# The first and second attention in one order of ticks, and the seams behind the second attention reordered

## Chip, core and metric

The kernel runs on one core of one Trainium2 chip. The metric is the device time of one execution in microseconds (us); the time before is the median of three runs. One more execution was profiled, and all rows of the trace come from that one.

## What is computed

A chain of four cross-attention blocks over x (8 sequences, 128 x 256) and a context of the same shape, all in fp32:

```python
x = L0(x, ctx)   # per (batch, head): softmax(q k) -> mean and deviation of v; out = instance_norm(x) * std + mean
x = L1(ctx, x)   # keys from [ctx, x]; 16 heads; then rmsnorm, gelu MLP, + residual
x = L2(x, ctx)   # layernorm, cross attention (16 heads of 128, one bias key), twice; then layernorm, MLP
x = L3(x, ctx)   # layernorm, cross attention, layernorm, gelu MLP
```

L0's deviation is `sqrt(relu(softmax @ (v*v) - mean*mean))`. L1 takes L0's output both as latents (queries, part of the keys) and as residual, so its projections need L0's rows of the batch at hand and no others.

## The kernel before

Every engine runs the same list of events, made by Python generators, and picks out its own part of each event; so the order of the list is the order of every engine's queue. TensorE (PE) multiplies, ScalarE (ACT) does exponentials and one half of the PSUM copies, VectorE (DVE) maxima, reciprocals and the other half, GpSimd (POOL) scales the probabilities, adds rows and clears buffers, SyncE (SP) issues the DMAs. A dense product in fp32 accuracy is three matmuls of rounded parts (helper `three`, lines 686 to 690), so L688, L689 and L690 are most of PE's work whatever the stage.

- **First attention (L0)**: `l0_order` puts events at ticks. Ticks 0 to 127 have one score unit S each; X (transposed scores, their exp is line 1292) follows nine ticks later, then PV (line 1026), N and OUT for the mean and second moment, and `vr` (lines 1796 to 1798) for the variance. Only when all is done come the `fin` events: per pair of rows a square root on ACT (line 1271), a product on POOL (line 1802), a sum and a mask on DVE (lines 1644 and 1645), and the transposes `nT lat` (line 711) that make L1's input.
- **Second attention (L1)**: `att_order("L1")`, a plain sequence behind L0: a head of dense products and stackings (dk, dq, dv, pq, pk), then 64 units S, T, PV (score line 800, exp 1155, scaling on POOL 1718, transpose 812, product 833), OUT and the output product WO after every 16 units, and the norm's steps nS (statistics, sqrt), nX (scaling), nT (transposes). `zero_keys` and `zero_values` (lines 1722, 1723, 1726) clear buffers of L1 on POOL behind `fin`. DVE runs it through `late`, which puts a few kinds of event behind the next score.
- **MLPs**: `mlp_order`: up and down products; a down's bank is one of the two general banks (`j_bank`, `j_full`, `j_take`), which all dense products share in turn and which are handed on only when the last user has emptied them.
- **Wide attention (L2)**: `wide_order`: 16 pairs of heads, eight units S (line 881), T (890), PV (903) each. The products q, k and v of pair p+1 and the output product WO of pair p-1 fill the ticks of pair p. Pairs 7 and 15 end a layer (`last`).
- **Third MLP and last attention (L3)**: `mlp_order("L2")`, `att_order("L3")`, `mlp_order("L3")`. `take` (lines 1081 and 1350) splits a loaded weight pack into its two rounded parts.
- Banks: L0's scores use PSUM banks 0, 1, 5, X 2 and 3, PV 4; L1 uses 0 and 1 for scores, 2 and 3 for transposes, 4 and 5 for outputs; 6 and 7 are the general banks.

## Time and profile before

| | before |
|---|---|
| median of 3 runs | 1208.99 us (1207.41 to 1210.04) |
| the profiled execution | 1209.98 us, its span 1208.2 us |
| mean granted TensorE clock | 0.964 of full speed |
| busy: PE, PEld, DVE, ACT, POOL | 1073.6, 947.2, 747.4, 731.9, 319.4 us |

PE is the matmul engine, PEld its weight loads, which overlap. The granted clock is 1.00 at 2.4 GHz and 0.50 at 1.2 GHz. "Idle" in a row's brackets is the engine's idle time just before that row, with what ended it.

### The profile page before, as it was taken

How to read it: one execution, taken by the hardware profiler on the slowest of the kernel's cores; microseconds unless marked ns; L12 is line 12 of the kernel's file. 1: busy time of each engine (PE TensorE's matmuls, PEld its weight loads, DVE VectorE, ACT ScalarE, POOL GpSimd, SP SyncE). 2: the span in 40 equal slices, each digit the busy share in tenths (PEclk: the TensorE clock that was granted, in tenths of full speed). 3: DMA queues.
4: the chain of work that ended last, by engine and by line, in shares of the span. 5: the costliest groups of instructions: out<-in, count | busy, mean ns of one | idle time of the engine just before them, and what ended most of it. 6: DMA issues, size and time to landing. Idle time of an engine off the chain costs nothing.

```text
span 1208.2 us, 23834 instructions
## 1 busy us (share of the span) xinstructions
PE 1073.6 (89%) x8224; PEld 947.2 (78%) x8224; DVE 747.4 (62%) x1777; ACT 731.9 (61%) x2114; POOL 319.4 (26%) x435
## 2 busy tenths in 40 slices
PE   3799995899978999999999889999999789688788
PEld 3577773777757989999999869999999679566688
DVE  4777775687886645555555745555555666566773
ACT  1577774678885446665666556666655442688842
POOL 5334335456441003211111112111111211243410
PEclk9899997999998999999999999999999889799899
DMA  6111110000001021100011111111001110100000
GB/s 202 26 28 45 45 28 36 1 1 2 19 19 44 19 88 45 42 29 26 37 45 66 45 44 45 44 45 44 32 28 40 36 36 1 36 2 19 19 10 27
DMA packets 20412, 43.65 MB, mean 36 GB/s; under 512 B 3395, under 2 KB 10821, under 8 KB 20294
## 3 DMA queue, kind: packets, MB, share of 16 engines
q1 hardware_dynamic: 20294, 42.12, 10.5%
q8 instruction: 68, 1.11, 0.4%
q14 instruction: 50, 0.41, 0.1%
HBM read 36.87 MB, written 1.05 MB: 31 GB/s over the span
## 4 chain that ended last, share of the span: by engine, by line
PE 69%; DVE 13%; ACT 9%; issue 6%; POOL 3%; DMA 0%; SPq 0%; DVEq 0%; ACTq 0%; POOLq 0%
PE ps L688 15%; PE ps L689 14%; PE ps L690 14%; PE ps L903 4%; PE ps L881 4%; PE ps L1026 2%; ACT pt L1155 2%; PE ps L890 2%; PE ps L812 2%; DVE nm L1667 2%; PE ps L1013 2%; PE ps L1004 1%; PE ps L833 1%; PE ps L769 1%; DVE nmax L1491 1%
## 5 line engine op out<-in xcount | busy, mean ns | idle before, releaser
L1718 POOL TENSOR_TENSOR pt<-pt,prec 128x256 f32<-128x256 f32 (+1 forms) x224 | 181.3, 810 | 650.4 <-DVE prec L1558 497.4
L1208 ACT ACTIVATE pt<-ps,nmax 128x129 f32<-128x129 f32 x256 | 92.4, 367 | 100.0 <-DVE nmax L1550 99.4
L688 PE MATMUL ps<-rs 128*128 128x256 f32 x480 | 144.7, 301 | 8.7 <-DVE rs L1572 3.9
L1350 DVE TENSOR_TENSOR rs<-wraw,rs 128x256 fp32r<-128x256 f32 (+2 forms) x116 | 67.5, 585 | 124.9 <-ACT rs L1081 124.2
L689 PE MATMUL ps<-rs 128*128 128x256 f32 x480 | 137.4, 286 | 0.0
L690 PE MATMUL ps<-rs 128*128 128x256 f32 x480 | 137.4, 286 | 0.0
L1155 ACT ACTIVATE pt<-ps,nmax 128x256 f32<-128x256 f32 (+1 forms) x256 | 105.3, 424 | 35.9 <-DVE nmax L1491 27.9
L688 PE MATMUL ps<-ht,rs 128*128 128x256 f32 (+1 forms) x304 | 108.6, 357 | 8.5 <-DVE X L1511 3.1
L688 PEld LDWEIGHTS ps<-rs 128*128 128x128 f32 x480 | 93.8, 195 | 13.0 <-DVE rs L1572 6.2
L689 PE MATMUL ps<-ht,rs 128*128 128x256 f32 (+1 forms) x304 | 102.1, 336 | 0.0
L690 PE MATMUL ps<-ht,rs 128*128 128x256 f32 (+1 forms) x304 | 101.9, 335 | 0.0
L689 PEld LDWEIGHTS ps<-rs 128*128 128x128 f32 x480 | 93.9, 196 | 0.0
L690 PEld LDWEIGHTS ps<-rs 128*128 128x128 f32 x480 | 93.6, 195 | 0.0
L1572 DVE SCALAR_TENSOR_TENSOR rs<-ps,col,rs 128x256 fp32r<-128x256 f32 x128 | 61.8, 483 | 49.5 <-ACT rs L1225 49.5
L688 PE MATMUL ps<-rs,ct 128*128 128x256 f32 x288 | 87.3, 303 | 3.2 <-ACT fs L1191 1.4
L1667 DVE TENSOR_REDUCE nm<-ps 128x2 f32<-128x512 f32 x128 | 81.8, 679 | 7.7 <-PE ps L1004 7.7
L1491 DVE TENSOR_REDUCE nmax<-ps 128x2 f32<-128x512 f32 (+1 forms) x96 | 66.0, 688 | 31.6 <-PE ps L804 26.7
L1251 ACT ACTIVATE fs<-ps,col 128x256 f32<-128x256 f32 x96 | 40.2, 472 | 73.1 <-PE ps L690 73.0
L881 PEld LDWEIGHTS ps<-fs 128*128 128x128 f32 x512 | 76.1, 191 | 10.2
L690 PE MATMUL ps<-rs,ct 128*128 128x256 f32 x288 | 81.4, 283 | 0.0
L689 PE MATMUL ps<-rs,ct 128*128 128x256 f32 x288 | 81.3, 282 | 0.0
L1292 ACT ACTIVATE pt<-ps 128x512 f32<-128x512 f32 x128 | 73.3, 598 | 12.8 <-PE ps L1013 10.7
(207 smaller groups left out, 3057.1 us busy)
## 6 DMA issues: line engine op xcount, KB each, us to landing
wraw<-in_packs SPq DMA_DIRECT2D x53, 512.0 KB, 3.5
bvr<-in_l2rows SPq DMA_DIRECT2D x16, 256.0 KB, 4.5
rs<-rs SPq DMA_DIRECT2D x80, 32.0 KB, 1.8
ht<-rs SPq DMA_DIRECT2D x48, 32.0 KB, 1.9
row<-in_rows SPq DMA_DIRECT2D x2, 640.0 KB, 5.4
XH<-in_packs SPq DMA_DIRECT2D x2, 512.0 KB, 4.2
out<-X SPq DMA_DIRECT2D x4, 256.0 KB, 2.1
X<-in_x SPq DMA_DIRECT2D x1, 768.0 KB, 7.1
```

The lines of the kernel that those rows point to most:

```text
L688: nc.tensor.matmul(dst, w[0], m[1], start=start, stop=False)
L689: nc.tensor.matmul(dst, w[1], m[0], start=False, stop=False)
L690: return nc.tensor.matmul(dst, w[0], m[0], start=False, stop=stop)
L881: last = nc.tensor.matmul(ps[:, S_BANK + g % 2, b * D:b * D + P + 1], qT[:, hh % 3, 2 * b2 + b, :], kT[:, hh % 3, 2 * b2 + b, :], start=Tr ...
L1155: last = nc.scalar.activation(prob[:, i % 3, h * keys:(h + 1) * keys], ps[:, SCORE_BANKS[ph][i % len(SCORE_BANKS[ph])], h * keys:(h + 1) * ...
L1208: last = nc.scalar.activation(prob[:, g % 3, k * D:k * D + P + 1], ps[:, S_BANK + g % 2, k * D:k * D + P + 1], ACT.Exp, bias=nmax[:, g % 4 ...
L1292: nc.scalar.activation(pt[:, i % L0_PTS, :], ps[:, L0_X[i % len(L0_X)], :], ACT.Exp, scale=Q0_SCALE).then_inc(Z["ex"], 1)
L1350: last = nc.vector.tensor_tensor(dst[1], src, f32(dst[0]), ALU.subtract)
L1491: nc.vector.tensor_reduce(nmax[:, i % 4, 0:nh], ps[:, SCORE_BANKS[ph][i % len(SCORE_BANKS[ph])], :].rearrange("p (h n) -> p h n", h=nh), A ...
L1572: nc.vector.scalar_tensor_tensor(cc[1][:, hd, two, :], ps[:, O_BANK + g % 2, 0:D].rearrange("p (b n) -> p b n", b=2), C(f"L2bv{p // PAIRS ...
L1667: nc.vector.tensor_reduce(nm[:, s % 3, im, 2 * p:2 * p + 2], ps[:, L0_S[i % len(L0_S)], :].rearrange("p (h n) -> p h n", h=2), AX.X, ALU.m ...
L1718: nc.gpsimd.tensor_tensor(pr, pr, prec[:, u % 4, 0:nh].unsqueeze(2).broadcast_to([P, nh, keys]), ALU.mult)\
```

## The change

`first_order` is now one list of ticks for L0 and L1, and `l0_order` is gone. Its core:

```diff
+L1_START = 140
-def l0_order():
+def first_order():
...
-    for k in range(3):
-        put(L0_UNITS + L0_LAG + 8 + k, "fin", k)
...
+    put(119, "w", "L1sel0")
+    put(121, "w", "L1sel1")
+    for k, (dev, mul, res, lat) in enumerate([(84, 87, 92, 119), (None, 91, 97, 123), (150, 152, 155, 160), (None, 154, 158, 164)]):
+        if dev:
+            put(dev, "dev", k // 2)
+        put(mul, "mul", k)
+        put(res, "res", k)
+        put(lat, "nT", "lat", k)
+    put(131, "zk", 0)
+    put(138, "zk", 1)
+    put(141, "zv", 0)
...
+    for tick, e in zip((130, 131, 133, 145, 147, 134, 135, 137), head, strict=True):
+        put(tick, *e, st="L1")
+    for u, events in enumerate(units):
+        for e in events:
+            put(L1_START + 2 * u, *e, st="L1")
```

`dev` is a square root over four rows at once (two of them instead of four `fin` roots), `mul` and `res` are the POOL and DVE parts of `fin`, `zk` and `zv` the clearing of L1's keys and values. L1's head stands at ticks 130 to 147 (dk, dq, dk, dv, dv, pq, pk, pk), its unit u at tick 140 + 2u. To make room, two of L0's key block buffers move out of `ht`, L1's probability buffers use slots L0 has freed, and waits on L0's semaphores guard the shared banks and slots. The rows that L1 adds to its residual on POOL come at units 4 to 7 and 14 to 17 (before, 1 to 8).

```diff
-    first, rest, sqrt = {"L1": (total - 24, total - 5, 6), "L3": (10, total - 3, 4)}[ph]
+    first, rest, sqrt = {"L1": (total - 24, total - 4, 10), "L3": (10, total - 3, 5)}[ph]
...
-        put(total - sqrt + 2 + n, "nT", after, k)
+        put(total - sqrt + 3 + (3 if ph == "L1" else 1) * n, "nT", after, k)
...
-            if w == (it + 1) * per_it + (WO_LATE if ph == "L3" and it + 1 < c["iters"] else 0):
+            if w == (it + 1) * per_it + ((WO_LATE if ph == "L3" else 1) if it + 1 < c["iters"] else 0):
```

In `wide_order`, the products for the second half of the batches of pairs 7 and 15 move from the pair before into the pair's own first ticks:

```diff
-            if not last and 4 <= u < 8:
+            if not last and 4 <= u < 8 and not ((p + 1) % PAIRS == PAIRS - 1 and u > 4):
                 yield ("v", p + 1, u - 4)
+            if last and u < 3:
+                yield ("v", p, u + 1)
...
-            if not last and u < 8:
+            if not last and u < 8 and not ((p + 1) % PAIRS == PAIRS - 1 and u % 2):
                 yield ("qk"[u // 2 % 2], p + 1, u // 4, u % 2)
+            if last and u < 4:
+                yield ("qk"[u % 2], p, u // 2, 1)
...
             else:
+                yield ("nX", norm, 1)
                 yield ("w", "L2w2_0", 0, PARTS)
-                yield ("w", "L2w2_1", 0, PARTS)
```

The take of L2w2_1 follows behind L2's second up product. At the end of the third MLP:

```diff
-    yield ("down", B // 2 - 1)
     if name == "L2":
         yield ("w", "L3att0", 0, PARTS)
         yield ("w", "L3att1", 0, PARTS)
+        yield ("half", B // 2 - 1)
+        yield ("nT", "L3n1", 0)
+    yield ("down", B // 2 - 1)
```

`half` is the first of the two batches of the last down product; the ACT wait of the takes for that product is gone. All down products now write to bank 0 or 1 (`S_BANK + c % 2`), with a semaphore of their own, and no longer take part in the round of the general banks.

## Rows read from the trace of the kernel before

**Rows 1.** The page: the chain that ended last, shares of the span by engine
```profile
PE 69%; DVE 13%; ACT 9%; issue 6%; POOL 3%; DMA 0%; SPq 0%; DVEq 0%; ACTq 0%; POOLq 0%
```
**Rows 2.** Busy time by stretch (start:end, us of stretch), granted clock behind POOL
```profile
core 0: us, PE busy (x) PEld busy (x) DVE busy (x) ACT busy (x) POOL busy (x), PEclk, DMA share, GB/s
100.00:140.00 40.00, 38.36 (x334) 30.36 (x332) 28.71 (x70) 29.74 (x56) 15.74 (x35) 1.00 0.15 41
191.80:225.80 34.00, 19.23 (x126) 15.71 (x126) 17.54 (x37) 11.54 (x23) 14.47 (x10) 0.70 0.09 31
260.00:320.00 60.00, 54.99 (x534) 45.14 (x533) 47.54 (x108) 46.33 (x147) 32.13 (x34) 1.00 0.01 2
500.00:600.00 100.00, 100.00 (x714) 93.34 (x714) 54.88 (x139) 60.35 (x198) 17.71 (x27) 1.00 0.11 41
```
**Rows 3.** Timeline between the attentions (start, us, engine line, [idle before])
```profile
191.84 1.93 PE L1026 MATMUL ps<-pt,fs 128*32 128x256 f32 x32 [0.69 <-ACT pt L1292]
197.59 0.61 POOL L1796 TENSOR_TENSOR fs<-fs 128x256 f32<-128x256 f32 x1 [9.07 <-ACT fs L1301]
199.92 4.15 POOL L1802 TENSOR_TENSOR X<-X,fs 128x512 f32<-128x512 f32 x3
208.73 3.51 POOL L1726 MEMSET fs<- 128x4096 f32 x1
214.74 0.69 ACT L1121 ACTIVATE rs<-ps,col 128x512 fp32r<-128x512 f32 x1 [1.92 <-PE ps L690]
225.85 0.47 PE L800 MATMUL ps<-rs 128*128 128x512 f32 x1 [0.97 <-DVE rs L1482]
231.57 1.04 POOL L1718 TENSOR_TENSOR pt<-pt,prec 128x512 f32<-128x512 f32 x1
244.34 1.04 POOL L1718 TENSOR_TENSOR pt<-pt,prec 128x512 f32<-128x512 f32 x1 [0.47 <-DVE prec L1436]
```
**Rows 4.** Timeline: a root among L0's exponentials, on ACT and PE
```profile
52.48 1.28 ACT L1275 ACT_TABLE_LOAD   x1
54.09 1.28 ACT L1292 ACT_TABLE_LOAD   x1
55.23 0.41 PE L996 MATMUL ps<-rs 128*128 128x128 f32 x2 [1.45 <-DVE fs L1686]
```
**Rows 5.** Who PE waited for, 230 to 350 us (total, times, longest)
```profile
PE ps L688 <- DVE rs L1505: 3.8, 3, 1.3
```
**Rows 6.** Timeline at L1's end
```profile
358.41 0.65 PE L833 MATMUL ps<-pt,fs 128*32 128x128 f32 x16 [0.53 <-DVE pt L1502]
364.61 1.08 PE L833 MATMUL ps<-pt,fs 128*32 128x128 f32 x16 [3.45 <-DVE pt L1502]
```
**Rows 7.** Timeline of pair 7, PE rows with idle time before them
```profile
664.65 0.38 PE L688 MATMUL ps<-rs 128*128 128x256 f32 x1 [0.80 <-DVE rs L1572]
667.87 0.39 PE L688 MATMUL ps<-rs 128*128 128x256 f32 x1 [0.42 <-DVE rs L1572]
...
688.33 0.44 PE L890 MATMUL ps<-ident,pt 128*128 128x128 f32 x2 [1.24 <-POOL pt L1718]
```
**Rows 8.** Timeline between wide attention and third MLP
```profile
973.53 2.36 DVE L1350 TENSOR_TENSOR rs<-wraw,rs 128x1024 fp32r<-128x1024 f32 x2 [1.37 <-ACT rs L1081]
974.39 1.28 ACT L1251 ACT_TABLE_LOAD   x1
978.72 1.09 PE L711 MATMUL ps<-ident,XH 128*128 128x128 f32 x4 [5.36 <-DVE XH L1386]
```
**Rows 9.** Timeline between third MLP and last attention
```profile
1021.08 3.52 POOL L1726 MEMSET fs<- 128x4096 f32 x1 [38.85 <-DVE rs L1594]
1021.47 3.15 DVE L1377 COPY sd<-mv 128x6 f32<-128x6 f32 x1
1026.10 0.63 PE L711 MATMUL ps<-ident,XH 128*128 128x128 f32 x4 [1.17 <-DVE XH L1386]
1031.56 0.55 PE L688 MATMUL ps<-ct,rs 128*128 128x256 f32 x1 [4.83 <-DVE rs L1350]
```

More of the change, by code:

```diff
@@ L96, with put @@
 NORMS = ["ctx", "lat", "L1r", "L2n1", "L2n2", "L2nm", "L3n1", "L3nm"]
-def l0_order():
+def first_order():
     at = {}
-    def put(tick, *e):
-        at.setdefault(tick, []).append(e)
+    def put(tick, *e, st="L0"):
+        at.setdefault(tick, []).append((st, *e))
     for s in range(L0_STEPS):
@@ L129, in l0_order @@
     put(52, "w", "L1att1")
-    for k in range(3):
-        put(L0_UNITS + L0_LAG + 8 + k, "fin", k)
-    yield ("dq", 0)
-    yield ("dl", 0)
-    yield ("pp", 0)
-    yield ("pp", 1)
-    yield ("dv", 0)
-    yield ("vq", 0)
+    put(119, "w", "L1sel0")
[9 more added lines that the diff above has]
+    put(141, "zv", 0)
+    head, units = [], []
+    for e in att_order("L1"):
+        if e[0] == "S":
+            units.append([])
+        (units[-1] if units else head).append(e)
+    for tick, e in zip((130, 131, 133, 145, 147, 134, 135, 137), head, strict=True):
[3 more added lines that the diff above has]
+            put(L1_START + 2 * u, *e, st="L1")
+    for e in ("dq", "dl", "pp"):
+        yield ("L0", e, 0)
+    yield ("L0", "pp", 1)
+    for e in ("dv", "vq"):
+        yield ("L0", e, 0)
     for u in range(max(at) + 1):
@@ L140, in l0_order @@
         if u < L0_UNITS:
-            yield ("S", u)
+            yield ("L0", "S", u)
         if 0 <= u - L0_LAG < L0_UNITS:
-            yield ("X", u - L0_LAG)
-    yield ("nT", "lat", 0)
-    yield ("fin", 3)
-    for k in range(1, B // 2):
-        yield ("nT", "lat", k)
+            yield ("L0", "X", u - L0_LAG)
 def att_order(ph):
@@ L551, in build @@
         L = {n: sem(f"L2_{n}") for n in ("qk", "v", "bv", "sm", "mx", "ex", "rc", "nm", "tm", "teA", "teD", "pm", "ch", "cl", "acc")}
-        M = {m: {n: sem(f"{m}_{n}") for n in ("gelu", "lo", "out")} for m in ("L1m", "L2m", "L3m")}
+        M = {m: {n: sem(f"{m}_{n}") for n in ("gelu", "lo", "dn", "out")} for m in ("L1m", "L2m", "L3m")}
         N = {n: {k: sem(f"{n}_{k}") for k in (["hi", "lo"] if n in ("ctx", "lat") else ["stat", "sq", "r", "xh", "a", "lo"])}
@@ L938, in mlp @@
                     j_full(last, (m["gelu"], (FT // 2) * c + f2 + 1))
-                elif e[0] == "down":
+                elif e[0] in ("half", "down"):
                     c = e[1]
@@ L943, in mlp @@
                         taken(pe, name + "w2_1")
-                    bank = j_bank()
-                    for b in range(2):
+                    if c >= 2:
+                        pe.wait_ge(m["out"], c - 1)
+                    bank = ps[:, S_BANK + c % 2, :]
+                    split = (name, c) == ("L2", B // 2 - 1)
+                    for b in (0,) if e[0] == "half" else (1,) if split else (0, 1):
                         for f in range(FT):
@@ L950, in mlp @@
                                          both(lambda i: mw2[name][i][:, f, :]), f == 0, f == FT - 1)
-                    j_full(last, (m["out"], c + 1))
+                    if e[0] == "down":
+                        last.then_inc(m["dn"], 1)
             def l0(e, i, *k):
@@ L957, in l0 @@
                     return
-                if e in ("w", "fin", "dl", "vq", "vr"):
+                if e in ("w", "sq", "dev", "mul", "res", "zk", "zv", "dl", "vq", "vr"):
                     return
@@ L1232, in mlp @@
                 func = ACT.Gelu if name == "L2" else ACT.Gelu_apprx_tanh
-                if e[0] == "down":
-                    j_skip()
+                if e[0] in ("half", "down"):
                     return
@@ L1637, in l0 @@
                     nc.vector.reciprocal(sd[:, 3, :], sd[:, 1, :]).then_inc(l0n, 1)
[L1638 to L1641 removed]
+                elif e == "res":
                     two = slice(2 * i, 2 * i + 2)
```

89 lines of the change are left out of this document (53 added, 36 removed).

## The prediction, made before the changed kernel ran

> **What bounds the kernel now.** I read the chain that ended last first. TensorE (PE) holds 69% of it, VectorE (DVE) 13%, ScalarE (ACT) 9% [rows 1]; so what can be won is PE's idle time, and time in which it runs at its lower clock level. The busy time by stretch then says where that is. In the first attention PE is busy 38.36 of 40 us, in the second 54.99 of 60, in the wide attention 100 of 100 [rows 2]. There a reordering wins nothing: in the first attention every microsecond added to PE is paid. Between the two attentions, from 191.8 to 225.8, PE is busy for 19.23 of 34.0 us at a mean granted clock of 0.70 of full speed [rows 2]. Its idle time there is 14.8 us, and the work would be shorter at full clock by about 0.3 x 19.2 = 5.8: 20.6 us is a hard bound on what this seam can give. The timeline shows why it is empty: last exponential, PV, two rounds of PSUM copies, variance on GpSimd (POOL), root on ACT, product, sum, transposes, and then the second attention's dense head, one after the other [rows 3]. The later seams have smaller holes: 3.45 us at the second attention's end [rows 6], 5.36 in front of the third MLP [rows 8], 1.17 and 4.83 in front of the last attention [rows 9].
>
> All sums stand against the profiled execution, 1209.98 us (span 1208.2, so 1.8 lie around the span); the median is 1.0 lower, which I leave out.
>
> **Part 1, the merged order.** I take one point that both kernels must pass, the start of POOL's tenth scaling (unit 9 of the second attention), at 244.34 in the trace [rows 3], and work out when it comes.
>
> (a) The tail of the first attention. The last PV starts at 191.84 [rows 3], eight exponentials behind the score units' end. The change puts dk, dq, dk, pq, pk, pk into this stretch. Their PSUM copies on ACT cost about 0.69 each [rows 3], 6 x 0.69 = 4.1, and PE's part (three products of 12 matmuls at 100/714 = 0.14 us each [rows 2], 5.0, and three small ones) runs beside that. With one wait for a general bank I take +5.2: PV at 197.0. The bound below is +2 (ACT's own idle time absorbs half), the one above +7 (nothing overlaps).
>
> (b) From PV to POOL. Before, PV to the start of the variance took 197.59 - 191.84 = 5.75 [rows 3]. Now the first two score units stand among these steps on DVE and ACT: I add 1.0, which is 203.9.
>
> (c) POOL's queue. Behind unit 0's scaling stand, in this order, `zv` (it waits for the last OUT copy), unit 1's scaling, `vr` of the last batch, unit 2's scaling. That is 3.51 + 1.04 + (199.92 - 197.59 = 2.33) + the gaps, some 0.6: unit 2's scaling starts at 211.4 [rows 3]. The dense values dv wait for `zv` on DVE, and the next score maxima stand behind them in DVE's queue; this lies beside POOL's own delay. Before, unit 2 started at 231.57. From unit 2 to unit 9 the rows give 244.34 - 231.57 = 12.77 for seven units [rows 3]. Taking the same pace, unit 9 starts at 224.2, 20.1 us earlier. That all but equals the hard bound, since the costs of (d) and (e) are still to come off.
>
> (d) What the moved steps cost inside the first attention, all of it on PE, which has no room there [rows 2]. `dev` at tick 84 is a table load, a root over 1024 columns and the load back. The trace has a like event: loads at 52.48 and 54.09, ACT blocked from 52.48 to 55.37, PE idle 1.45 us [rows 4] and slower just after. The new root is longer (1024 columns against 8; 512 columns pass ACT in 0.69 [rows 3], so about 0.8 to 1.1 more), some 3.7 us of ACT, of which PE loses 3.0 (between 1.45 and 3.7). The transposes `nT lat` 0 and 1 are 0.6 each on PE [rows 9], 1.2. Two `res` on DVE (two operations of 512 columns each, estimated at 1.4 together by ACT's 0.69) hit score maxima that have three banks of slack: 0.3 to 1.5, I take 0.9. The two products on POOL (4.15/3 = 1.4 each [rows 3]) are hidden, POOL being busy 15.74 of 40 us [rows 2]; if they delay the small casts for the next step they cost up to 1 each. No DMA moves: SyncE's list keeps its order. Sum 5.1, between 3 and 8.
>
> (e) In the shared stage: the second `dev` (3.7 us of ACT, mostly beside POOL's delay), two products, two `res`, two `nT lat`. I take 2.0, between 0 and 6.
>
> Seam: -20.1 + 5.1 + 2.0 = -13.0 us, between -20 and -4.
>
> Of a table switch the trace shows 0.02 us between the load's end and the root (load of 1.28 at 52.48, the two loads 1.61 apart with the root between [rows 4]). The Trainium skill (ScalarE: Activation LUTs, What ACT_TABLE_LOAD costs) adds a drain of about 1.38 us to every load, 2.66 in all; with four switches where two were, this would speak against the change by some 5 us. By that page the sum would be some 5 us later; the trace does not agree with it, so I leave it out.
>
> **Part 2, the second attention.** WO one unit later: PE stood three times before it, 3.8 us in all [rows 5]; now another unit's work lies between. As others are near their limit I take -2.0 (0 to -3.8). At the end, the norm's root moves up four units and now stands right behind the third WO: ACT waits there for PE's product, DVE's sum and statistics, about 1 us more than the old hole, and everything queued behind it on ACT, the next exponential first, waits too. In return the transposes are spread three units apart, so that DVE's casts for them no longer pile up ahead of the probability copy PE waited 3.45 and 0.53 us for [rows 6]; the product that came out of the long wait took 1.08 where its like took 0.65 [rows 6], the lower clock level, which cost some 3 us more. I take -3.0 (-7 to +2).
>
> **Part 3, the wide attention.** PE has nothing to win in the steady pairs [rows 2]. In pair 7 it stood 0.80 and twice 0.42 us before WO [rows 7], because there was no q or k product behind PV to cover the copies. The moved products cover these: -1.6 per layer. But they leave pair 6 without cover: WO after two of its odd ticks now stands in the same way (0.8 and 0.4), and ticks 5 and 7 have only S, T and PV, about 1 us of PE work, against the chain through maximum, exponential and scaling (the thinnest tick of pair 7 stood 1.24 us for POOL's scaling [rows 7]); 2 x 0.9, between 0.5 and 1.24 each. Net +1.4 per layer at most, -1.6 at best; I take +1.0, +2.0 for both layers.
>
> **Part 4, in front of the third MLP.** PE stood 5.36 us for the second half's nX, which DVE did only behind 2.36 us of weight splitting, itself waiting for ACT [rows 8]. Now nX comes first and one of the two splits later. What is late next is the general bank: the transposes need the first gelu, behind one cast of weights and the table load. The load started at 974.39 [rows 8] and now starts 1.0 us earlier; its gelu ends near 975.5, so PE goes on there instead of at 978.72. That is -3.0; the split that is put off comes back on DVE later (0 to -5).
>
> **Part 5, in front of the last attention.** The takes no longer wait for the last product, so PE's 4.83 us before the first dense product [rows 9] goes. But PE now does half of the last product and then waits for nX, since the transposes stand in front of the second half. nX cannot come sooner: DVE's copy of the variances took 3.15 us under POOL's clearing of 3.52 [rows 9]. PE arrives about 2.9 us earlier at a wait that ends at the same 1026.10, then has 0.6 and 24 matmuls to do (3.4 us at the mean of [rows 2], less the wide ones in that mean, 2.9), and the dense head starts at 1029.6 instead of 1031.56: -2.0 (-4 to +1). The same clearing in (c) now runs among the second attention's copies. The Trainium skill (SBUF — State Buffer, Who interferes with whom) says that a GpSimd instruction and a DVE copy in a two-port mode exclude each other for a whole instruction; the 3.15 us row agrees with it.
>
> The down products' own banks take away a wait or two at a norm: -1.0 (0 to -2). The root one unit earlier in L3: nothing measurable, its transposes stay where they are.
>
> **Sum.** -13.0 - 2.0 - 3.0 + 2.0 - 3.0 - 2.0 - 1.0 = -22.0: 1209.98 - 22.0 = 1188.0 us.
>
> **The rivals.**
> *The seams close fully.* ACT's idle time absorbs the head, (d) and (e) come at their lower ends (-20.1 + 3 + 0 = -17), the end of the second attention gives -6, pair 6 costs nothing. -17 - 3 - 6 + 0 - 4 - 3 - 2 = -35: 1175. For it speaks that ACT was busy only 11.54 of the 34 us [rows 2]; against it, that PE's queue is one list and any late event holds all behind it.
> *POOL's clearing inside running work.* Three clearings (one of 3.51 us for 4096 columns [rows 3], so two of 1.8 for 2048) stand among DVE copies that they hold up as in [rows 9]: up to 7.1 us, and pairs 6 and 14 cost their +2.8. -22 + 7 + 1 + 2 for a longer (e) = -12: 1198.
> *The order does not do what it says.* If the first scores could not start before all of the first attention's chain is through, only the head's dense work (5 to 8 us) would overlap, less (d): 1203. Against it: the rows' products and transposes 0 and 1 need nothing of the last batches.
> *Slower: the clock.* PE in the merged stretch waits behind POOL again and again; if the granted clock falls to the half level and stays there through the second attention, its work takes 1.08/0.65 = 1.7 times as long [rows 6]. From 22/0.7 = 31 us of PE work at that level the gain is gone; at 45 us it is 1209.98 - 22 + 31 = 1219. Against it: at 92% busy the second attention held 1.00 throughout [rows 2].
>
> **Chances.** Forecast (1181 to 1195) 0.48, full closing (1170 to 1181) 0.21, POOL's clearing (1195 to 1201) 0.19, no real overlap (1201 to 1208) 0.07, clock 0.05. The range that leaves out 2 in 10 reaches into both neighbours: 1172 to 1200. Both signs do not share the chance, so no second range is needed. A difference of 0.2%, 2.4 us, is about what a measurement of this kernel can tell from no change. Faster 0.93, same 0.02, slower 0.05.
>
> **What would show each step.** (a) to (c): the last PV (line 1026 now) near 202 with (d) in it, and POOL's tenth scaling near 231. (d): a hole on ACT of about 3.7 us near 130 with PE idle 2 to 3 us beside it. Part 2: no idle before WO, the wait before the last PVs under 2 us. Part 3: no idle before WO in pair 7, short waits in pair 6's odd ticks. Part 4: a wait of about 2.5 us before the transposes in place of 5.36. Part 5: one wait of 4 us between the halves, none before the dense head. Wrong would be the forecast above all if POOL's queue did not hold units 1 and 2, or if the clock fell in the stages behind.

## The result, and the profile after

The changed kernel took 1204.61 us (median of 8 runs, 1202.46 to 1206.83), the kernel before beside it 1209.64 (1207.11 to 1211.03): a ratio of 0.9961, 95% interval 0.9951 to 0.9972. It is 5 us faster; the forecast was 22 us, and its range, 1172 to 1200, does not hold the result. The profiled execution has a span of 1205.0 us (before 1208.2).

The chain that ended last has moved little: 65% PE where it was 69%, and one point more each for DVE, ACT and issue [rows 1].

```profile
PE 65%; DVE 14%; ACT 10%; issue 7%; POOL 3%; DMA 0%; DVEq 0%; SPq 0%; ACTq 0%; POOLq 0%
```

The timeline of the seam (start, us, engine, line), with the rows that answer to [rows 3]: last PV, the POOL queue, first score block, tenth scaling.

```profile
209.62 1.94 PE L1053 MATMUL ps<-pt,fs 128*32 128x256 f32 x32 [0.64 <-ACT pt L1321]
212.68 0.48 PE L816 MATMUL ps<-rs 128*128 128x512 f32 x1
...
215.81 1.04 POOL L1749 TENSOR_TENSOR pt<-pt,prec 128x512 f32<-128x512 f32 x1 [5.54 <-DVE prec L1465]
216.78 3.52 POOL L1757 MEMSET fs<- 128x4096 f32 x1
220.26 1.04 POOL L1749 TENSOR_TENSOR pt<-pt,prec 128x512 f32<-128x512 f32 x1
221.26 0.61 POOL L1830 TENSOR_TENSOR fs<-fs 128x256 f32<-128x256 f32 x1
...
223.60 3.04 POOL L1749 TENSOR_TENSOR pt<-pt,prec 128x512 f32<-128x512 f32 x3
...
245.43 1.04 POOL L1749 TENSOR_TENSOR pt<-pt,prec 128x512 f32<-128x512 f32 x1 [3.92 <-DVE prec L1465]
```

The order is the one that the forecast read out of the diff: clearing, scaling 1, variance, scaling 2. The last PV came at 209.6 instead of the forecast's 202, and the tenth scaling at 245.4 instead of 231. In front of the seam, ScalarE's first stop, which is the new root `dev` of the first half's rows between two table loads, and PE behind it (ACT, then PE rows):

```profile
138.70 1.28 ACT L1300 ACT_TABLE_LOAD   x1
139.99 1.06 ACT L1300 ACTIVATE fs<-fs 128x1024 f32<-128x1024 f32 x1
141.06 1.28 ACT L1321 ACT_TABLE_LOAD   x1
142.36 0.60 ACT L1321 ACTIVATE pt<-ps 128x512 f32<-128x512 f32 x1
...
143.01 0.80 PE L1040 MATMUL ps<-rs 128*128 128x256 f32 x2 [2.55 <-ACT pt L1321]
```

ACT is away for 142.36 - 138.70 = 3.66 us, as forecast (3.7). PE stands for 2.55 of them, and the first product behind the hole takes 0.80 us, where its like at full clock takes 0.40. Behind the seam, PE's larger waits in the second attention's first twelve units:

```profile
230.02 0.50 PE L816 MATMUL ps<-rs 128*128 128x512 f32 x1 [2.09 <-ACT pt L1184]
242.36 0.66 PE L725 MATMUL ps<-ident,X 128*128 128x128 f32 x4 [2.44 <-ACT rs L1170]
250.50 0.71 PE L776 MATMUL ps<-rs,sel 128*128 128x256 f32 x4 [1.59 <-DVE rs L1476]
```

The first is the second root. The second are the transposes of the third row pair, which wait until ACT has copied stacked keys out of a bank. The third is the stacking of the queries, behind DVE's correction of a key product. In the wide attention, PE was busy throughout pair 6 before (first line, the window of pair 6 in the kernel before). The second line is a window of like length in the changed kernel, pair 6 and the first ticks of pair 7; under it stand two PE rows of it:

```profile
628.90:660.40 31.50, 31.50 (x226) 29.37 (x225) 17.15 (x43) 19.14 (x62) 5.02 (x8) 1.00 0.18 64
627.80:659.40 31.60, 26.93 (x199) 24.56 (x198) 16.93 (x45) 18.00 (x65) 5.62 (x9) 1.00 0.17 64
...
648.98 0.44 PE L911 MATMUL ps<-ident,pt 128*128 128x128 f32 x2 [1.14 <-POOL pt L1749]
654.77 0.44 PE L911 MATMUL ps<-ident,pt 128*128 128x128 f32 x2 [1.90 <-POOL pt L1749]
```

And in front of the third MLP and the last attention, the waits that stand in the place of [rows 8] and [rows 9]:

```profile
979.95 0.66 PE L725 MATMUL ps<-ident,XH 128*128 128x128 f32 x4 [2.51 <-ACT fs L1279]
...
1022.00 3.51 POOL L1757 MEMSET fs<- 128x4096 f32 x1 [40.03 <-DVE rs L1625]
1022.40 3.14 DVE L1406 COPY sd<-mv 128x6 f32<-128x6 f32 x1
1027.02 1.09 PE L725 MATMUL ps<-ident,XH 128*128 128x128 f32 x4 [4.04 <-DVE XH L1415]
```

These two are what the forecast asked for: 2.51 in place of 5.36, and one wait of 4.04 in place of 1.17 and 4.83.

**How the stretches are measured below.** Every kernel passes the same marks: first attention's score block 24, its last one (127), the second attention's score blocks 0, 16, 24 and 52, the wide attention's first. I take the stretches between them, because an execution can fall up to 3 us behind near 50 us, ahead of score block 24, whatever the kernel (block 24 starts between 57.6 and 60.4 us over all kernels here; in the profile of after it was 60.3, before 57.7). A mark is the start of that score block in the PE rows; every trace here has all 128 blocks of the first attention and all 64 of the second. In the tables, Z is a score block of the first attention and S one of the second. Each stretch is from one profiled execution per kernel, and the ratios are from several timed ones.

### The profile page after: what moved, and what is told of

The parts are those of the page before. It is cut to its first block, busy times and chain, and to the rows that moved or that the text cites. A ratio compares the mean times of both kernels' runs of the same rounds, so it can differ in the third digit from the quotient of the medians.

```text
span 1205.0 us, 23843 instructions
## 1 busy us (share of the span) xinstructions
PE 1072.2 (89%) x8224; PEld 944.0 (78%) x8224; DVE 746.2 (62%) x1777; ACT 731.5 (61%) x2114; POOL 321.7 (27%) x435
## 4 chain that ended last, share of the span: by engine, by line
PE 65%; DVE 14%; ACT 10%; issue 7%; POOL 3%; DMA 0%; DVEq 0%; SPq 0%; ACTq 0%; POOLq 0%
PE ps L702 14%; PE ps L703 13%; PE ps L704 13%; PE ps L926 4%; PE ps L902 4%; PE ps L1053 3%; ACT pt L1184 2%; PE ps L911 2%; DVE nm L1698 2%; PE ps L830 2%; DVE nmax L1520 1%; PE ps L1040 1%; PE ps L1031 1%; PE ps L853 1%; PE ps L783 1%
## 5 line engine op out<-in xcount | busy, mean ns | idle before, releaser
L702 PEld LDWEIGHTS ps<-rs 128*128 128x128 f32 x480 | 92.7, 193 | 7.5 <-DVE rs L1603 5.3
L703 PEld LDWEIGHTS ps<-rs 128*128 128x128 f32 x480 | 92.8, 193 | 0.0
L704 PEld LDWEIGHTS ps<-rs 128*128 128x128 f32 x480 | 92.7, 193 | 0.0
```

The lines of the kernel that those rows point to most:

```text
L702: nc.tensor.matmul(dst, w[0], m[1], start=start, stop=False)
L703: nc.tensor.matmul(dst, w[1], m[0], start=False, stop=False)
L704: return nc.tensor.matmul(dst, w[0], m[0], start=False, stop=stop)
```

## The experiments

**The changed kernel once more**, nothing edited.

> The changed kernel once more, unchanged. In its first profile score block 17 of the first attention (about 50 us) already stands 2.75 us later than in the kernel before, although nothing in the program differs up to there. Theory A (a half-clock stretch that falls differently from execution to execution): score block 17 comes back to within 0.5 us of before, and the span ends about 1202. Theory B (the new order itself does it, for instance by where its instructions lie): 2.75 us again, span 1204 to 1206. Both expect the last weighted sum of the first attention at 206 to 210 us and the tenth scaling of the second attention at 242 to 246 us.

It took 1203.83 us; score block 24 came at 59.2, and from block 30 on it stood 0.5 us behind the kernel before, where the first profile stood 3.0 behind. That is theory A. From block 24 to 127 it took 130.1 us where the first profile has 134.0 and before 125.3; from block 127 to the tenth scaling 51.2 in both. So the first attention's loss varies from execution to execution, the seam does not. The first profile had bad luck there: 3.9 us in this stretch alone.

**The wide edit undone, and alone.** Undone in the changed kernel (r2), and the only edit in the kernel before (r3):

```diff
-            if not last and 4 <= u < 8 and not ((p + 1) % PAIRS == PAIRS - 1 and u > 4):
+            if not last and 4 <= u < 8:
-            if last and u < 3:
-                yield ("v", p, u + 1)
-            if not last and u < 8 and not ((p + 1) % PAIRS == PAIRS - 1 and u % 2):
+            if not last and u < 8:
-            if last and u < 4:
-                yield ("qk"[u % 2], p, u // 2, 1)
```

> The changed kernel with one part undone: the projections of the last pair of each wide-attention layer go back to where the kernel before has them. Forecast before the result: this edit costs 2.0 us in all. Theory A, from the two profiles (the wide layers took 6.6 us longer after): the edit itself costs 6.6 us, in the pairs ahead of the last, where the score ticks have less matmul work and the weighted sums wait for POOL's scaling (1.14 and 1.90 us at 649 and 655 us); then this kernel takes 1198 us, 0.990 to 0.992 of before. Theory B: the wide layers are slower because of what else moved (the buffers of the second attention, one MLP's banks); then nothing changes, 1204 to 1205 us. Theory C, my forecast of 2.0: 1202.5.

> The kernel before with one part of the change alone: the projections of the last pair of each wide-attention layer moved. Theory A (the edit costs 6.6 us whatever stands around it): 1216 us, 1.0055 of before. Theory B (the loss in the wide layers comes from other parts): 1209.6, no change. My forecast: 1211.6.

Undone: 1199.91 us, 0.9907 (0.9888 to 0.9926) of before, where the changed kernel has 0.9961: 6.5 us by the ratios. Alone: 1215.59, 1.0038 (1.0025 to 1.0051), 4.6 us slower. So the edit costs by itself, as theory A had it, but A's 6.6 us lie outside the interval of the edit alone. From the wide attention's first score block to the transposes behind its first layer: before 246.7 us, undone 246.7, alone 251.6, changed 250.2, and 251.8 in r1.

**Its two halves**, each alone on the kernel of r2. The v products (r9) keep the first two edits above, the q and k products (r10) the last two.

> The kernel with the wide edit undone, but with the v products of the last pair moved as in the change (the q and k products stay). Theory A (the loss is pair 6's thin score ticks: only ticks that lose both a v product and a q or k product stand on POOL's scaling, as at 648.98 and 654.77 us for 1.14 and 1.90 us): each tick of pair 6 keeps its q or k product, so no wait and no half clock there; 0 to 1.5 us slower or faster, ratio to before 0.990 to 0.992. Theory B (any product taken out of a pair in which PE is busy for all of its 31.6 us costs about its own share of the 4.6 us): half of it, 0.9925.

> The kernel with the wide edit undone, but with the q and k products of the last pair moved as in the change (the v products stay). Theory A: ticks 1 and 3 of pair 6 keep nothing between transposes and weighted sum, ticks 5 and 7 keep a v product, so one or two waits of 0.3 to 1.2 us a layer; pair 7's waits before WO shrink by as much; ratio to before 0.990 to 0.993. Theory B (half of the 4.6 us): 0.9925.

Ratios 0.9911 (0.9896 to 0.9927) and 0.9906 (0.9889 to 0.9924); the same stretch took 248.3 and 246.9 us. The halves cost 1.6 and 0.2 us in this layer, both together 3.5 to 5.1. The ratios can't tell the theories apart, since both intervals reach B's 0.9925 or end beside it. The stretches are for theory A: what costs is a score tick that has lost both products. In r9 the waits for POOL behind pair 6's ticks 5 and 7 are 0.20 and 0.52 us, in the changed kernel and in r3 1.14 and 1.90. Behind the 1.90 the granted clock of the next 5 us was 0.66 in r1 and r3, the ones with 251.8 and 251.6, and 1.00 in the first profile of the changed kernel and in r4, which have 250.2. The rows of r9:

```profile
651.17 0.44 PE L908 MATMUL ps<-ident,pt 128*128 128x128 f32 x2 [0.20 <-POOL pt L1746]
654.58 0.44 PE L908 MATMUL ps<-ident,pt 128*128 128x128 f32 x2 [0.52 <-POOL pt L1746]
```

A thin tick is not enough, though. From the first layer's transposes to those behind the second layer, the kernels without any part of the edit took 269.9 to 273.3 us, those with all of it 272.4 to 274.1: little or nothing lost, though pair 14 is thinned in the same way. In the changed kernel PE waited there 0.17 and 0.56 us in the place of 1.14 and 1.90. The difference stands in DVE's queue. In pair 6 the score maximum, on which exponential and scaling hang, comes behind a weight split (line 1379) that waits for ACT's cast (first two rows); in pair 14 no split stands at ticks 5 to 7, and the maximum comes as soon as its scores are there (third row, then PE's two waits):

```profile
647.40 0.43 DVE L1379 TENSOR_TENSOR rs<-wraw,rs 128x256 fp32r<-128x256 f32 x1 [1.48 <-ACT rs L1108]
647.74 0.42 DVE L1581 TENSOR_REDUCE nmax<-ps 128x2 f32<-128x258 f32 x1
...
920.67 0.43 DVE L1581 TENSOR_REDUCE nmax<-ps 128x2 f32<-128x258 f32 x1 [0.84 <-PE ps L902]
...
921.91 0.44 PE L911 MATMUL ps<-ident,pt 128*128 128x128 f32 x2 [0.17 <-POOL pt L1749]
926.30 0.44 PE L911 MATMUL ps<-ident,pt 128*128 128x128 f32 x2 [0.56 <-POOL pt L1749]
```

No run moves the split, so this is read from the trace and not tested.

**The later seams alone, and the merge alone**, on the kernel before. r5 holds the second attention's WO and norm, the seams in front of the third MLP and the last attention, and the down products' own banks; r6 holds the merged order with the buffers and waits that it needs.

> The kernel before with the reordering of the later seams alone (the second attention's WO and norm, the third MLP's norm, the last attention's start, the down products' own banks), without the merged order and without the wide layers' edit. Theory A (the merge gave next to nothing, the later seams carry the whole gain): by the marks of the two profiles they are worth 1.0 + 1.7 + 4.9 + 2.5 + 1.0 = 11.1 us, so 0.991 of before, as much as merge and later seams gave together in the kernel with the wide edit undone (0.9907). Theory B (my forecast's sizes: 2.0 + 3.0 + 3.0 + 2.0 + 1.0): 11.0 us too, so the sum can't tell, but the parts do: A has 4.9 in front of the third MLP and 1.7 at the second attention's end. Theory C (the later seams give less without the merge, because something there hangs on it): over 0.994.

> The kernel before with the merged order of first and second attention alone. Theory A (what the seam gives is taken back by what stands in the way of PE in the first attention and in the second's first 16 units): between 2 us faster and 1 us slower, 0.998 to 1.001 of before. My forecast's size was 13.0 us faster, 0.989. Marks that A expects: first score block of the second attention 15 to 18 us earlier than before, its seventeenth 0 to 4 us earlier.

Later seams: 1202.20 us, 0.9937 (0.9923 to 0.995). Merge: 1207.76, 0.9986 (0.9976 to 0.9997). The later seams give less than the 11 us of theories A and B; in front of the third MLP they give B's size (3.0) and not A's 4.9, as the marks below show. The merge is within theory A's 0.998 to 1.001. In microseconds of 1209.3: -7.6, -1.7, and +4.6 for the wide edit. The sum is -4.7, and the changed kernel measured 0.9961, which is -4.7: the three parts add, as far as intervals of 1.3 to 1.6 us each way can tell. The merge, forecast at -13, gives 1.7.

**The price of the roots.** The two new steps of ScalarE pass the variance through:

```diff
-                    nc.scalar.activation(dev, dev, ACT.Sqrt).then_inc(l0dev, 1)
+                    nc.scalar.activation(dev, dev, ACT.Identity).then_inc(l0dev, 1)
```

> The changed kernel without the square root of the deviation: both new ScalarE steps (at 139 and 226 us) pass the variance through unchanged, so no table of the square root is loaded; this leaves out that root. It prices the two steps. Theory A (a stop of ScalarE for 3.65 us in a stretch where the matmul engine is busy costs the whole stop and a half-clock stretch behind it): 5.3 us back at the first, at least 3.6 us at the second, since the matmul engine idles 2.09 us at 230 us and runs at half clock from 231 to 234; the time is 1195 to 1197 us. Theory B (the second is hidden, because POOL's queue sets the order of the scalings from 220 to 252 us anyway): only the first counts, or even it is taken back at POOL; 1199 to 1203 us.

1197.56 us, 0.9886 (0.986 to 0.9912). The first root's price can be read block by block. I subtract the starts of the first attention's score blocks in the kernel before; the difference is steady from block 30 to 86 and from 90 to 94, and the root stands between. It grew by 5.2 us there in the first profile of the changed kernel, and by nothing in r4. In all twelve kernels that have this root at this place, ScalarE stopped for 3.66 us and PE for 2.55, yet the price came in three sizes, and it goes with the granted clock of PE's next 5 us: 2.9 us where the clock was 1.00 (r1, r10, r11, r15, r17), 4.4 where it was 0.67 to 0.69 (r2, r7, r8, r9, r16), 5.1 and 5.2 where it was 0.50 (r6, after). The mean is 3.9. In r1 and in r2, PE's row behind the hole and the five microseconds from it:

```profile
140.41 0.51 PE L1040 MATMUL ps<-rs 128*128 128x256 f32 x2 [2.55 <-ACT pt L1321]
140.41:145.41 5.00, 4.67 (x49) 3.18 (x49) 2.08 (x3) 3.76 (x7) 2.97 (x5) 1.00 0.16 35
```

```profile
140.63 0.51 PE L1033 MATMUL ps<-rs 128*128 128x256 f32 x2 [2.55 <-ACT pt L1314]
140.63:145.63 5.00, 4.67 (x28) 3.46 (x32) 2.08 (x3) 3.87 (x7) 2.93 (x5) 0.69 0.13 30
```

From block 94 to 127 the difference grew by another 3.1 us in each of them, and in r4 too: 1.3 up to block 100, where the products and sums stand, and 1.8 from block 118 on, where the transposes, the casts of `L1sel` and the second attention's first events stand. In the second attention, block 0 to 24 took 58.8 instead of 61.4 (r2): the second root costs 2.6, less than theory A's 3.6. Theory B, that it is hidden, falls too.

**Bare stops in the kernel before.** Nothing else added:

```diff
+                    for j in ({24: (8,), 44: range(9, 16)}.get(i, ()) if ph == "L1" else ()):
+                        nc.scalar.activation(junk[:, j, :], ident[:, 0:16], ACT.Sqrt)
...
+                    for j in {60: (0,), 100: range(1, 8)}.get(i, ()):
+                        nc.scalar.activation(junk[:, j, :], ident[:, 0:16], ACT.Sqrt)
```

> The kernel before with four added stops of ScalarE and nothing else: table load, roots of 16 columns into an unused tile, table load back. One root (a stop of about 2.8 us) at score block 60 of the first attention and at block 24 of the second; seven roots (about 4 to 4.5 us) at block 100 of the first and block 44 of the second. Theory A (PE has some 1 us of slack in front of ScalarE, pays the rest of the stop and a half-clock stretch behind it): 2 to 3 us for a short stop, 4 to 6 for a long one, in either attention; 12 to 18 us in all, ratio 1.010 to 1.015. Theory B (my forecast's rate, 3.0 us for a stop of 3.7): 1.5 to 2.3 short and 3.0 to 3.6 long, 9 to 12 us in all. Theory C (the second attention has more slack, being 92% busy): nearly nothing for the short stop there.

1228.10 us, 1.014 (1.0125 to 1.0156), 17 us for four stops. Each is read off the score blocks around it, whose distance to the kernel before is steady in between: from 1.7 to 5.8 and 5.8 to 11.5 in the first attention, 10.5 to 14.2 and 14.2 to 19.4 in the second. Timeline of the long one in the first attention (ACT, then PE), and busy time of the five microseconds of each stop and the five behind it, short stop first:

```profile
171.27 1.28 ACT L1296 ACT_TABLE_LOAD   x1
172.56 0.85 ACT L1296 ACTIVATE junk<-ident 128x16 f32<-128x16 f32 x7
173.42 1.28 ACT L1297 ACT_TABLE_LOAD   x1
...
175.36 0.80 PE L1014 MATMUL ps<-rs 128*128 128x256 f32 x2 [2.81 <-ACT pt L1297]
...
119.20:124.20 5.00, 2.19 (x12) 1.76 (x12) 2.70 (x5) 4.80 (x8) 3.17 (x5) 0.92 0.11 26
124.20:129.20 5.00, 5.00 (x48) 3.35 (x48) 1.12 (x2) 2.36 (x5) 0.00 (x0) 0.74 0.11 26
...
171.20:176.20 5.00, 2.19 (x12) 1.54 (x9) 2.12 (x4) 4.96 (x14) 0.74 (x3) 0.84 0.11 26
176.20:181.20 5.00, 5.00 (x31) 3.85 (x34) 1.87 (x4) 2.48 (x5) 1.86 (x3) 0.50 0.04 10
```

| stop | ScalarE away | PE idle | granted clock in the 5 us behind | cost |
|---|---|---|---|---|
| first attention, short | 2.80 us | 2.81 | 0.74 | 4.1 us |
| first attention, long | 3.44 | 2.81 | 0.50 | 5.6 |
| second attention, short | 2.81 | 2.75 | 0.72 | 3.7 |
| second attention, long | 3.45 | 2.72 | 0.54 | 5.2 |

PE's hole is no shorter than ScalarE's stop is for the short ones, and behind it PE is busy for 5 of 5 us at a lower clock: 0.26 x 5 = 1.3 and 2.8 + 1.3 = 4.1; 0.5 x 5 = 2.5 and 2.8 + 2.5 = 5.3, near the 5.6. Theory A holds, even above its size for the short stops; theories B and C fall. These are single executions, and the three sizes of the root's price above say that another one could have another clock behind the same hole. So the difference between short and long stop here is not shown to come from the length. The forecast's 3.0 was PE's hole without the clock behind it.

**Where the moved steps stand.** On the kernel of r2: the second half (root, products, sums, transposes of rows 4 to 7) late (r7), almost without work (r8), spread (r11); and the first half behind the last score block (r12); r14 joins r11 and r12.

```diff
-[(84, 87, 92, 119), (None, 91, 97, 123), (150, 152, 155, 160), (None, 154, 158, 164)]
+[(84, 87, 92, 119), (None, 91, 97, 123), (162, 164, 167, 172), (None, 166, 171, 176)]   r7
+[(84, 87, 92, 119), (None, 91, 97, 123), (152, 158, 163, 170), (None, 176, 182, 190)]   r11
+[(129, 130, 131, 134), (None, 131, 132, 150), (152, 154, 157, 162), (None, 156, 160, 166)]   r12
+[(129, 130, 131, 134), (None, 131, 132, 150), (152, 158, 163, 170), (None, 176, 182, 190)]   r14
```

> The kernel with the wide edit undone, and the second half of the first attention's rows (root, product, sum, transposes of row pairs 2 and 3) moved from units 5 to 12 of the second attention to units 11 to 18. Theory A (the 9 us between the third and the tenth scaling go to these steps because they meet the start, where scores, dense product and POOL's backlog already wait for one another; later the queues have slack): the stretch from the third scaling to the tenth takes 13 to 15 us instead of 21.8, at most 4 us come back at units 11 to 18, and the kernel gains 4 to 6 us, 0.986 to 0.988 of before. Theory B (the steps cost PE the same wherever they stand, since the second attention is 92% busy): the loss moves with them, 0.990 to 0.992. Theory C (POOL's clearing and the variance in front of scaling 2 are what delays the tenth scaling): the stretch stays near 20 us.

> The kernel with the wide edit undone, in which product and sum of row pairs 2 and 3 run over 8 columns instead of 256 for each row; this leaves out most of these rows' update. Order, waits, root and transposes stay. It prices the duration of these six instructions alone (POOL 1.28 and 1.72, DVE 1.51, 1.03, 0.84 and 1.04 us in the profile). Theory A (it is their length on DVE and POOL ahead of score maxima and scalings): third to tenth scaling 21.8 becomes 17 to 19 us. Theory B (it is the chain of waits, root to product to sum to transposes to their casts, each ending a wait on an engine that stands in front of the next unit's work): 20 to 21.5 us.

> The kernel with the wide edit undone, in which the second half of the first attention's rows is spread: root at unit 6 of the second attention, row pair 2 at units 9, 12 and 15, row pair 3 at units 18, 21 and 25. With it, the residual's rows go to units 16, 17, 28, 29 and 30 to 37. Theory A (these steps cost because they stand close together and wait for one another): second attention's 25th score block 3 us or more earlier against the first attention's last score block than the 79.9 us of before, ratio 0.987 to 0.989. Theory B (what they cost is their own time on engines that are full there, ScalarE 3.65 us, VectorE 4.4 us and the transposes with their casts, and it comes wherever they stand): no change against moving all of it late, 0.990 to 0.992, the 33rd score block 7 to 10 us behind what the pace of before would give.

> The kernel with the wide edit undone, in which the first half's root, products, sums and transposes no longer stand among the first attention's score blocks (84 to 123) but behind the last of them (129 to 134, the transposes of row pair 1 at 150), with the dense head of the second attention behind them. Theory A (in the first attention PE loses the whole price of ScalarE's stop, in the tail ScalarE has room beside PE): the stretch from score block 24 to the last goes from 132.6 back to 125 to 127 us, the first score block of the second attention comes 4 to 8 us later after it than the 18.5 us of before this edit, net 0 to 3 us gained, 0.988 to 0.991. Theory B (the chain root, product, sum, transposes, dense product, selection lies whole in front of the first score block): it comes 12 us or more later, and the kernel is slower than without this edit, 0.993 to 0.996.

> The kernel with the wide edit undone, with both placements: the first half's root and rows behind the first attention's last score block, the second half's spread over units 6 to 25 of the second attention. Theory A (the gains add): the first attention's score blocks as without the merge (24 to 127 in 125 to 127 us), 139 us from block 127 to the second attention's block 52 plus the 6 us that the late rows cost, 0.987 to 0.989 of before, the fastest so far. Theory B (in both placements the same work waits in ScalarE's and VectorE's queues, so the one undoes the other): 0.989 to 0.991.

Stretches in us, by first attention block (Z) and second attention block (S):

| kernel | Z24 to Z127 | Z127 to S0 | S0 to S24 | Z127 to S52 | ratio to before (95%) |
|---|---|---|---|---|---|
| before | 125.3 | 42.9 | 47.2 | 151.5 | 1 |
| later seams alone, r5 | 125.7 | 41.9 | 46.9 | 149.3 | 0.9937 (0.9923 to 0.995) |
| merge alone, r6 | 133.9 | 18.4 | 61.7 | 141.4 | 0.9986 (0.9976 to 0.9997) |
| wide edit undone, r2 | 132.6 | 18.4 | 61.4 | 140.5 | 0.9907 (0.9888 to 0.9926) |
| second half late, r7 | 132.7 | 18.4 | 61.2 | 140.2 | 0.9913 (0.99 to 0.9927) |
| second half tiny, r8 | 132.7 | 18.5 | 58.9 | 138.0 | 0.9899 (0.9886 to 0.9913) |
| second half spread, r11 | 131.5 | 18.5 | 58.5 | 139.2 | 0.9894 (0.9879 to 0.991) |
| first half late, r12 | 125.5 | 24.5 | 61.6 | 146.7 | 0.9889 (0.9871 to 0.9907) |
| both, r14 | 125.7 | 23.1 | 60.2 | 145.5 | 0.9907 (0.9891 to 0.9923) |

Moved late (r7), the stretch from the third to the tenth scaling fell from 21.8 to 12.5 us, which is what it took before (12.8): the whole loss in that stretch was these steps. But by block 24 all of it had come back: 61.2 against 61.4. That is theory B. The length of the product and sum instructions is 2.5 us (r8); third to tenth scaling took 19.4 us there, between r8's two theories and nearer A. Spread over 20 units (r11), the second attention's block 24 came 2.9 us earlier behind block 127 than in r2, but block 52 only 1.3; the ratio lies between both theories, so neither is shown. The first half behind the blocks (r12) gives the first attention its 6 to 7 us back and takes 6.0 in front of S0. From Z24 to S52 that is 272.2 us against 273.1 in r2, within the 0 to 3 us that theory A had; A's ratio fits as well. With both moves (r14), the marks are those of theory A (125.7 and 145.5) and the ratio is that of theory B, so this stays open. The ratios of these kernels differ by less than their intervals are wide.

**POOL's clearing**, shortened to 64 columns (r15), and in eight pieces of 512 columns (r16; r17 has the spread order too):

```diff
-                nc.gpsimd.memset(fs[:, 0:4096], 0.0).then_inc(vzero, 1)
+                for j in range(7):
+                    link(nc.gpsimd.memset(fs[:, 512 * j:512 * (j + 1)], 0.0))
+                nc.gpsimd.memset(fs[:, 3584:4096], 0.0).then_inc(vzero, 1)
```

> The kernel with the wide edit undone, in which POOL's clearing of the value tile covers 64 of its 4096 columns; this leaves out the zeros between the heads' values, so the second and third attention add up old contents too. Theory A (the clearing stands in POOL's queue between the first and the second scaling and costs its 3.5 us there): third scaling 10 to 11 us after the first attention's last output copy instead of 11 to 12 minus nothing, that is first score block to third scaling 10.9 becomes 7.4 us, and 2.5 to 3.5 us gained at unit 16. Theory B (beside it DVE and ACT do the dense head's copies, which are as late): under 1.5 us gained at unit 16. The clearing ahead of the third attention is short too, worth 0 to 2 us there.

> The kernel with the wide edit undone, with POOL's clearing of 4096 columns written as eight instructions of 512 columns, the same work. Theory A (VectorE's small copy is held up for the rest of the one long instruction beside it): in front of the last attention the copy ends within 0.6 us instead of 3.14, the transposes behind it start 2 to 3 us earlier, ratio to before 0.988 to 0.989 against 0.9907. Theory B (the copy is slowed by any clearing beside it, however cut, until all is through): copy again 3 us, no gain, and at the first seam 0 to 1 us lost by the gaps between the pieces.

> The clearing in pieces together with the second half's rows spread over units 6 to 25 of the second attention, the wide edit undone. If the two gains are independent (0.9894 against 0.9907, and 2 to 3 us for the pieces): 0.9865 to 0.988, 1193 to 1195 us, the fastest. If theory B of the run beside it holds: 0.989 to 0.990.

Shortened: 1195.18 us, 0.9871 (0.9847 to 0.9895). At the first seam the third scaling came 1.5 us earlier behind block 127 (27.9 instead of 29.4), the tenth at 51.2 as in r2: no gain there, theory B. The gain is in front of the last attention: from the wide attention's first block to the third attention's first it took 587.6 us against 592.5 in r2. In pieces it took 589.8. In the timeline of r16, DVE's copy, the pieces and PE's wait:

```profile
1015.51 0.17 DVE L1399 COPY sd<-mv 128x6 f32<-128x6 f32 x1
1015.11 4.12 POOL L1751 MEMSET fs<- 128x512 f32 x7 [40.05 <-DVE rs L1618]
1017.70 0.63 PE L721 MATMUL ps<-ident,XH 128*128 128x128 f32 x4 [1.61 <-DVE XH L1408]
```

The copy took 0.17 us although POOL was clearing beside it, and PE's wait was 1.61, where r2 has 3.14 and 4.04: the one long instruction holds the copy, not the clearing as such. That is theory A for the copy. The timed ratio of r16, 0.9905 (0.989 to 0.9919), is not A's 0.988 to 0.989: it shows nothing of the 2.7 us. A part went back at the first seam, where block 127 to block 52 took 141.4 us against 140.5 in r2, as theory B had it. r17 took 1196.76 us, 0.9888 (0.9873 to 0.9903), above the 0.9865 to 0.988 expected of two gains that add, and at the edge of theory B's 0.989. It has the lowest time of the kernels that do all the work, with r12's 0.9889 beside it, and is faster than the changed kernel by about 0.7%, since the intervals lie apart. Most of that is the wide edit that it leaves out.

## Why the prediction was wrong

**(a) to (c), from the last PV to the third scaling: right.** From block 127 to the third scaling, 48.6 us became 29.3, which is 19.3 less; the forecast was 20.2 less. By steps: the tail from block 127 to the last PV grew by 6.5 us (forecast 5.2), PV to POOL's clearing was 7.16 (6.9), clearing to third scaling 6.82 (7.5). That POOL's queue sets the tenth scaling, on which (c) rests, was not so: r15 took 3.4 us out of it and the tenth scaling did not move.

**(d), the moved steps inside the first attention: mis-sized.** Forecast 5.1, measured 3.9 + 3.1 = 7.0 in the mean, and 5.2 + 3.1 = 8.3 in the first profile. The term that failed is the root: 3.0 for a stop of 3.7 us. That is right to 0.1 us where the clock held, in five of twelve executions; in the other seven it was 4.4 to 5.2, and bare stops of 2.8 and 3.4 us cost 4.1 and 5.6 (r13). The rest, forecast at 2.1, was 3.1: products and sums 1.3 (forecast 0.9), the transposes with what stands beside them 1.8 (1.2). The forecast had read PE's idle 1.45 us beside a stop of 2.9 in [rows 4], and "slower just after", but gave the clock no number, though it stood in the trace: the window behind that stop in the kernel before, and behind the new one in the changed kernel:

```profile
55.20:60.20 5.00, 4.54 (x19) 3.73 (x19) 3.29 (x6) 3.87 (x8) 2.05 (x4) 0.66 0.11 26
```

```profile
143.00:148.00 5.00, 4.99 (x20) 4.00 (x24) 2.07 (x3) 3.71 (x7) 2.96 (x5) 0.50 0.13 29
```

0.34 x 4.5 = 1.5 us would have come on top of the 3.0.

**(e), the shared stage: this is the step that failed.** Forecast 2.0 with 6 as its upper end; from the third to the tenth scaling it was 21.8 us instead of 12.77, so 9.0. All of it is the second half's steps, for with them moved away it was 12.5 (r7). Its parts: the second root 2.6 (r4), the length of products and sums 2.5 (r8), together some 5; bunching about 1.3 (r11). The last 2 to 3 us, which hold two rounds of transposes with their casts, were not taken apart and stay open. "Mostly beside POOL's delay" was wrong: ACT, DVE and PE were busy for 46, 48 and 55 of 60 us in the second attention [rows 2], in one loop that hands each unit from one to the next. Moved late in that loop, the steps cost as much by block 24 (61.2 us against 61.4, r7); spread out, they cost 1.3 less (r11).

So the seam, forecast at -13.0, is -19.3 + 7.0 + 9.0 = -3.3 by the marks. Alone (r6) it gave -1.7 as timed; there the root fell into the dearest of its three sizes in the profile, and from Z24 to S52 it took 275.4 us against 276.8, which is -1.4.

**Part 2.** WO: block 16 to 52 took 77.78 us instead of 78.85, -1.1 (forecast -2.0). The second attention's end: block 52 to the wide attention's first, 110.7 instead of 112.0, -1.3 (forecast -3.0).

**Part 3, the wide attention: mis-sized.** Right in its mechanism, thin ticks that wait for POOL's scaling, down to pair 6's ticks 5 and 7. The size was +2.0, +1.0 a layer, and is +4.6 (r3): 3.5 to 5.1 in the first layer, little or nothing in the second. The forecast gave each thin tick 0.9 us from the thinnest of pair 7 (1.24). They took 1.14 and 1.90 in pair 6, with the lower clock behind the longer one in two of four profiles, and 0.17 and 0.56 in pair 14. By the reading above, what its chain of maximum, exponential and scaling left out is the weight split in DVE's queue ahead of the maximum, which pair 6 has and pair 14 has not.

**Parts 4 and 5: right.** Wide attention's first block to the second transposes in front of the third MLP, 532.3 to 529.7 us, -2.6, and -3.5 at the last (forecast -3.0); from there to the third attention -1.3 (forecast -2.0); behind it -1.2 (own banks, forecast -1.0). Parts 2, 4 and 5 together: -8.4 by the marks of r5, -7.6 as timed, forecast -11.0. A mark behind the second layer is good to 1 or 2 us only, since kernels that are alike up to there differ by as much.

**The rivals.** POOL's clearing, 1198 us, had the right sign of the miss and the wrong cause: at the seam the clearing cost nothing (r15). That the order would not do what it says was not so either: block 0 came 24.5 us sooner behind block 127. No rival held what happened, that the moved work comes out as time in loops whose PE looked 4 and 8% idle. The clock did fall, in short stretches behind holes, in some executions and not in others, and not for good.

## What to carry to other kernels

A gap closed by moving its work elsewhere gives only what the work costs less in its new place. Before counting a gain, price every moved instruction there, on each engine of the loop and not on the fullest alone: in a loop where three engines are busy 77 to 92% and wait for one another in turn, the moved work is not hidden. Price a stop of a feeding engine at PE's hole behind it plus what PE then loses at the lower clock. A bare stop in the unchanged kernel measures it, four prices in one run; but take several executions, because the clock behind one and the same hole differs from one to the next. Where PE is full, don't take work out of a tick that is only just covered, and look at what stands in the other engines' queues at that tick.

## What the runs showed of the hardware

- ScalarE's stop for a root among exponentials was 2.80 us with one root of 16 columns and 3.66 with one of 1024, from the first table load to the next exponential; between a load's end and the next activation lay 0.01 to 0.02 us. The stop of 3.66 cost the first attention 2.9 to 5.2 us and the second 2.6, bare stops of 2.80 to 3.45 cost 3.7 to 5.6.
- Behind one and the same hole of PE, 2.55 us long, at the same place of the first attention, the granted clock of the next 5 us was 1.00 of full speed in five executions, 0.67 to 0.69 in five and 0.50, the lower level, in two. What decides between them the runs don't tell. Behind the bare stops, with holes of 2.7 to 2.8 us, it was 0.50 to 0.74, in one execution each.
- A copy of 6 columns on DVE took 3.14 us beside one clearing of 4096 columns on POOL and 0.17 beside eight clearings of 512. The Trainium skill (SBUF — State Buffer, Who interferes with whom) says that of GpSimd and a VectorE copy in a two-port mode, whichever issues first keeps the shared port pair for its whole instruction and the other is blocked; the pieces agree with it. At the first seam the same clearing of 3.52 us held nothing up that counted: the tenth scaling did not move without it.
